# Feed-forward of a fused attention block: gate and up with the ternary weights stationary, the inner transposes gone, heads split a tile ahead, a new order on TensorE

## The reference

```python
def h_bitlinear(x, w):
    xq = act_quant(fwht(x))
    wq = weight_quant(w)
    return jnp.einsum('bsh,oh->bso', xq, wq)
gate = h_bitlinear(hidden_states, w_gate)
up = h_bitlinear(hidden_states, w_up)
return h_bitlinear(jax.nn.silu(gate) * up, w_down)
...
x = x + _L0_xattn_ref(_layernorm(x, axis=-1), ctx_1024, ...)
x = x + _L0_ffn_ref(_layernorm(x, axis=-1), ...)
```

## Time and profile before

| | |
|---|---|
| Median of 3 runs | 1412.14 us (1410.57 to 1414.44) |
| Profiled execution, own time | 1411.2 us |
| Its span | 1409.4 us |
| Mean granted TensorE clock | 0.996 |
| TensorE busy | 1378.7 us, 98% |
| VectorE, ScalarE, GpSimd busy | 934.5, 940.3, 516.6 us |

### The profile page before, as it was taken

How to read it: one execution, slowest core, us unless ns; L and a number is a source line. 1 busy time by engine, 2 the same in 40 slices (tenths; PEclk the granted TensorE clock), 3 DMA queues, 4 the chain that set the end, 5 groups by cost and what they waited for, 6 DMA issues and landing times. The chain is left out here.

```text
span 1409.4 us, 25806 instructions
## 1 busy us (share of the span) xinstructions
PE 1378.7 (98%) x8407; PEld 1187.5 (84%) x8407; DVE 934.5 (66%) x2399; ACT 940.3 (67%) x2072; POOL 516.6 (37%) x323
## 2 busy tenths in 40 slices
PE   8999988999999999999999999999989999999998
PEld 8889867999999999999999999998967676776765
DVE  5222046667777777777777777767457677776775
ACT  4566558888888888888888888888633334343332
POOL 0033324432233223332233223335544465655551
PEclk9999999999999999999999999999999999999999
DMA  7767813344433443444434444326343322233211
GB/s 234 213 180 221 232 48 90 91 122 118 130 111 116 131 130 108 112 135 117 125 108 123 125 128 124 105 82 190 123 153 88 78 61 68 61 98 75 60 30 42
DMA packets 173492, 165.05 MB, mean 117 GB/s; under 512 B 81440, under 2 KB 149040, under 8 KB 171568
## 3 DMA queue, kind: packets, MB, share of 16 engines
q1 hardware_dynamic: 166448, 150.82, 38.7%
q10 hardware_dynamic: 6912, 12.59, 2.7%
HBM read 123.44 MB, written 33.01 MB: 111 GB/s over the span
## 5 line engine op out<-in xcount | busy, mean ns | idle before, releaser
L768 POOL TENSOR_TENSOR rk_sp<-ms_sp,neg_half 76x10 f32<-76x10 f32 (+1 forms) x128 | 237.9, 1876 | 560.2 <-DMA ms_sp<-ms 560.2
L1198 DVE CUSTOM_DVE_ANT_0 sc<-psS,rk 100x361 f32<-100x361 f32 x256 | 136.5, 533 | 93.1 <-PE psS L843 71.5
L990 ACT ACTIVATE pr<-ex,ri 100x361 f32<-100x361 f32 x256 | 153.6, 600 | 63.4 <-DVE ri L1188 63.4
L983 ACT ACTIVATE ex<-sc,nb,rq_all 100x361 f32<-100x361 f32 x256 | 175.9, 687 | 5.5 <-DVE nb L1207 5.3
L871 PE MATMUL psZ<-pT_hi,cK_hi 120*128 120x400 f32 (+1 forms) x384 | 132.9, 346 | 0.0
L871 PE MATMUL psZ<-pT_hi,cK_lo 120*128 120x400 f32 (+1 forms) x384 | 131.8, 343 | 0.0
L871 PE MATMUL psZ<-pT_lo,cK_hi 120*128 120x400 f32 (+1 forms) x384 | 131.8, 343 | 0.0
L856 PEld LDWEIGHTS psP<-ident,pr 100*120 100x120 f32 (+1 forms) x768 | 80.2, 165 | 43.4 <-issue 35.3
L843 PE MATMUL psS<-ring_hi,q_hi 128*100 128x362 f32 x256 | 96.8, 378 | 4.3 <-DVE mx L1198 4.2
L856 PE MATMUL psP<-ident,pr 100*120 100x100 f32 (+1 forms) x768 | 96.5, 261 | 3.9 <-ACT pr L990 3.9
L1180 DVE TENSOR_TENSOR pT_lo<-psP,pT_hi 121x600 fp32r<-121x600 f32 x128 | 99.0, 774 | 1.5 <-ACT pT_hi L1014 1.3
(11 more groups left out here) (295 smaller groups left out, 3940.0 us busy)
## 6 DMA issues: line engine op xcount, KB each, us to landing
rk<-rk_dram SPq DMA_DIRECT2D x64, 564.1 KB
q_dram<-q_out SPq DMA_DIRECT2D x64, 200.0 KB, 4.6
q_in<-q_dram SPq DMA_DIRECT2D x64, 200.0 KB, 5.1
o_dram<-o SPq DMA_DIRECT2D x64, 200.0 KB, 5.4
stage<-in_w_ff SPq DMA_DIRECT2D x12, 1024.0 KB, 6.2
w_in<-in_w_ff ACTq DMA_DIRECT2D x48, 256.0 KB, 2.4
o_in<-o_dram SPq DMA_DIRECT2D x12, 1024.0 KB, 6.0
cT_in<-in_ctxT SPq DMA_DIRECT2D x15, 361.0 KB, 4.4
```

The source lines that it names most:

```text
L768: nc.gpsimd.tensor_tensor(rk_sp[:, cols], ms_sp[:, cols], neg_half[0:HG * SKR, :].to_broadcast([HG * SKR, n]), op=ALU.pow).then_inc(g_rk, 1)
L983: nc.scalar.activation(ex[:, h % 2, :], sc[:, h % 2, :], ACT.Exp, bias=nb[:, h % 2:h % 2 + 1], scale=factor(n), accum_out=rs[:, h % 2:h % ...
L990: nc.scalar.activation(pr[:, h, :], ex[:, h % 2, :], ACT.Copy, scale=ri[:, h % 2:h % 2 + 1]).then_inc(a_pr, 1)
L1198: nc.vector.tensor_tensor_reduce(out=sc[:, h % 2, :], in0=psS[0:SQ, 0:SK], in1=rk[:, u % 2, h, :], scale=1.0, scalar=-3.0e38, op0=ALU.mult ...
```

## The change

- **Gate and up.** The ternary weights are stationary, 128 x 128 at a time, and the 128 tokens of `q1T` move. Four matmuls of 512 columns become sixteen of 128. Hidden values now lie on the partitions and tokens along the columns, so `hidden_T` goes away. The scale of a token lies along the columns too: `al_T` transposes it (`al_rows`), ScalarE copies it to `alT`, VectorE multiplies gate by it (`gate`), ScalarE applies silu in SBUF, VectorE multiplies by up (`hidden`); the scale of up is folded into `scales2`.
- **Rotation.** `low_hT` reads `half_rot` and `hT_hi`, both in SBUF. GpSimd takes the inner rotation of blocks 0 and 1 one by one, and of the stage across only the difference of blocks 1 and 3; VectorE takes that of 0 and 2.
- **Heads.** The split of tile i+3 is used a step later: `out_high` (L1507) issues the two products with `o_hi` for heads 0 to 12 in one step and 13 to 15 in the next, `out_low` (L1514) the 16 with `o_lo` then. `low_o` waits for `v_hT`, the low parts of the hidden values of tile i+1.
- **Order.** TensorE rotates all four blocks ahead of `norm_T`; VectorE has the low parts ahead of norm and `rotate_halves`, and three peaks behind `low_xT`; GpSimd moves the residuals in the next step, after `v_q`. The fillers change.
- **Last tile.** 128 matmuls of 64 columns instead of 32 of 512 in column halves.

```diff
-        AHEAD, FIRST = 6, 10
+        AHEAD, FIRST = 13, 8
...
             def low_o(t):
                 pool.wait_ge(a_o, t + (NO - 1))
-                pool.wait_ge(v_xr, 2 * t - 2)
+                pool.wait_ge(v_hT, (t - 1) * NB)
                 nc.gpsimd.tensor_tensor(o_lo[:], o_in[:], o_hi[:].bitcast(F32), op=ALU.subtract).then_inc(g_o, 1)
...
             def rotate_across(t):
-                nc.gpsimd.tensor_tensor(half_rot[:, 2:4, :], hid[:, 0:2, :], hid[:, 2:4, :], op=ALU.subtract).then_inc(g_r2, 1)
+                nc.gpsimd.tensor_tensor(half_rot[:, 3, :], hid[:, 1, :], hid[:, 3, :], op=ALU.subtract).then_inc(g_r2, 1)
...
+                if i > -2:
+                    if 0 <= i and not last_tile(i):
+                        pool.wait_ge(v_q[1], 2 * i + 2)
+                    move_residuals(i - 1)
...
+            def out_high(t, heads):
+                if heads[0] == 0:
+                    pe.wait_ge(a_o, t + (NO - 1))
+                    pe.wait_ge(v_x1, t - 1)
+                for h in heads:
+                    for w in (wo_hi, wo_lo):
+                        nc.tensor.matmul(psA[:], o_hi[:, h, :], w[h // HALF][:, h % HALF, :],
+                                         start=(h == 0 and w is wo_hi), stop=False)
+            def out_low(t):
+                pe.wait_ge(g_o, t - 1)
+                for h in range(H):
+                    last = nc.tensor.matmul(psA[:], o_lo[:, h, :], wo_hi[h // HALF][:, h % HALF, :],
+                                            start=False, stop=(h == H - 1))
...
-                for k in range(2):
-                    for c in range(DC):
-                        last = nc.tensor.matmul(psB[:, 2 * (j % 2) + k, :], q1T[:, c, :],
-                                                wt[:, k, c, j * DIM:(j + 1) * DIM], start=(c == 0), stop=(c == DC - 1))
-                last.then_inc(p_gu, 1)
+                width, chunks = (TH, FC // 2) if last_tile(t) else (TT, FC // NB)
+                for k, done in enumerate((p_gate, p_up)):
+                    for i in range(chunks):
+                        col = (j * chunks + i) * P
+                        for c in range(DC):
+                            last = nc.tensor.matmul(psB[:, 2 * (j % 2) + k, i * width:(i + 1) * width], wt[:, k, c, col:col + P],
+                                                    q1T[:, c, 0:width], start=(c == 0), stop=(c == DC - 1))
+                    last.then_inc(done, 1)
...
-                nc.vector.tensor_tensor(hT_lo[:, n * DC:(n + 1) * DC, :].rearrange("p c t -> p (c t)"), psT[n % 2][:],
-                                        hT_hi[:, n * DC:(n + 1) * DC, :].rearrange("p c t -> p (c t)").bitcast(F32),
-                                        ALU.subtract).then_inc(v_hT, 1)
+                hi, lo = (a[:, n * DC:(n + 1) * DC, :].rearrange("p c t -> p (c t)") for a in (hT_hi, hT_lo))
+                nc.vector.tensor_tensor(lo, half_rot[:, 2 + n if last_tile(t) else n, :], hi.bitcast(F32), ALU.subtract
+                                        ).then_inc(v_hT, 1)
...
+            def gate(t, j):
+                nc.vector.tensor_tensor(sil[:, j % 2, :].rearrange("p (i t) -> p i t", t=width),
+                                        psB[:, 2 * (j % 2), :].rearrange("p (i t) -> p i t", t=width),
+                                        alT[:, 0:width].unsqueeze(1).to_broadcast([P, blocks, width]), ALU.mult).then_inc(v_g, 1)
```

More of the change, by code:

```diff
@@ L1304, in feed_forward @@
         a_o, v_o, g_o = s("a3_o"), s("v3_o"), s("g3_o")
-        p_out, p_xT, p_rx, p_q1T, p_gu, p_hT, p_rh, p_down = (
-            s(f"p3_{n}") for n in ("out", "xT", "rx", "q1T", "gu", "hT", "rh", "down"))
+        p_out, p_xT, p_rx, p_q1T, p_alT, p_gate, p_up, p_rh, p_down = (
+            s(f"p3_{n}") for n in ("out", "xT", "rx", "q1T", "alT", "gate", "up", "rh", "down"))
         v_x1, v_st, g_rs, v_xn, v_xr = (s(n) for n in ("v3_x1", "v3_st", "g3_rs", "v3_xn", "v3_xr"))
@@ L1483, in _, with first_out_proj @@
         def _(pe):
[L1484 to L1489, removed]
+            def first_out_proj(heads):
                 for h in heads:
-                    if first:
-                        pe.wait_ge(v_o, h // OH + 1)
+                    pe.wait_ge(v_o, h // OH + 1)
                     hi, lo = (w[h // HALF][:, h % HALF, :] for w in (wo_hi, wo_lo))
@@ L1648, in step @@
                         gate_up(i + 1, j)
-                if real(i + 2):
-                    out_proj(i + 2, range(FIRST if isinstance(i, int) and i == -1 else AHEAD, H))
-                if real(i + 1):
-                    hidden_T(i + 1, 0)
-                    hidden_T(i + 1, 1)
+                if isinstance(i, int) and i == -1:
+                    first_out_proj(range(FIRST, H))
+                    busy(psT[1], 8)
+                elif real(i + 2):
+                    out_high(i + 2, range(AHEAD, H))
+                    out_low(i + 2)
                 if real(i):
@@ L1669, in step @@
                 if real(i + 3):
-                    out_proj(i + 3, range(0, 4))
-                if isinstance(i, int) and i == TILES - 3:
+                    out_high(i + 3, range(3, 9))
+                elif i == TILES - 3:
                     busy(psA, 11)
@@ L1674, in step @@
                     q1_T(i + 2)
+                    al_T(i + 2)
                 if real(i + 3):
-                    out_proj(i + 3, range(4, AHEAD))
+                    out_high(i + 3, range(9, AHEAD))
+                elif i == TILES - 3:
+                    busy(psA, 3)
             busy(psT[1], 4)
@@ L1761, in step @@
                     if real(i + 1):
-                        silus(i + 1, (j,))
+                        silu(i + 1, j)
                 if real(i + 1):
-                    high_hT(i + 1, 0)
-                    high_hT(i + 1, 1)
+                    for n in range(NB):
+                        high_hT(i + 1, n)
                 if real(i + 3) and not (isinstance(i, int) and i == -2):
@@ L2019, in step @@
                 if real(i + 1):
-                    peak(i + 1, 2)
-                    peak(i + 1, 3)
+                    for n in range(1, NB):
+                        peak(i + 1, n)
                 if real(i + 2):
```

281 lines of the change are left out of this document (131 added, 150 removed).

## The result

The changed kernel takes 1489.60 us (median of 4, 1489.34 to 1495.81) against 1411.36 us of the kernel before measured beside it (1409.38 to 1414.44): a ratio of 1.0566, 95% interval 1.0552 to 1.0581. It is slower by 5.7%. The forecast was 1487. The profiled execution took 1489.68 us, with a span of 1487.9.

A forecast was written before the change was run, and what follows sets the result against it. TensorE, busy for 98% of the span, was taken as the bound. With -1.4 ahead, +5.5 first tile, +70 ten tiles, -0.4 twelfth and +2 half tile, +76 on 1411.2 gave 1487 us, range 1402 to 1500.

The forecast's parts named there:

- The added wait: Ahead of the normalised rows' transposition: GpSimd's split holds off both rotation halves, TensorE idle from 19.8 to 26.0 us.
- rival (a): The long split lets short VectorE operations through: a tile of 28.5 us, 1405 us in all; chance 0.24.
- TensorE's work: Per tile: gate and up +0.2 us, sixteen transposes leave -1.8, one for the scales +0.1; sum -1.4.
- the row of four: Four 128-column matmuls in the earlier trace, 0.40 us in all, 0.060 each; basis for taking 0.057.
- rival (c): Small gate and up matmuls cost more than 0.057 us, nothing blocks: 1450 us at 0.085 each; chance 0.05.
- VectorE's chain to the rotation: From the tile's first matmul to both rotation halves: ends at 20.5 us if unblocked, where TensorE wants them at 19.8.
- From there to the next tile: From the normalised rows' transposition to the next tile: 8.4 us, with a 0.65 us wait for the integers.
- rival (b): The split comes after the rotation anyway, as its input is late: 28.9 us a tile, 1409 us; chance 0.11.
- The clock: Half clock behind TensorE's idle time in each tile: from nothing to 3.4 us, taken as 1.7.
- The sum: Whole kernel: -1.4 ahead, first tile +5.5, ten tiles +70, twelfth -0.4, half tile +2; together +76 us, 1487 us.
- The half tile: Last half tile: 128 matmuls of 64 columns take 3.5 to 7.7 us, taken as +2.5; with -0.5 elsewhere, +2.
- The twelfth tile: The last whole tile, with no split behind it and fewer fillers: -0.4 us.

The follow-up runs named there:

- e1: The changed kernel with GpSimd's split of the heads waiting for both halves of the rotation again: 1425.43 us, ratio 1.0106.
- e2: The changed kernel with the split of the heads issued as four GpSimd operations of 512 columns: 1440.17 us, ratio 1.0209.
- e3: The kernel before, with the split of the heads waiting for the normalised rows and no longer for the rotation: 1458.09 us, ratio 1.0335.
- e9: e8 with the split of the heads waiting for the low parts of the hidden values again, as in the change: 1472.94 us, ratio 1.0445.
- e8: e7 with the second half of the hidden values' integers behind the next tile's first gate product on VectorE: 1405.40 us, ratio 0.9949.
- e4: The changed kernel with 20 unread matmuls per tile added in TensorE's wait ahead of the transposition of the normalised rows: 1478.08 us, ratio 1.0474.
- e6: e5 with 11 heads of the output projection ahead of a tile instead of 13: 1424.38 us, ratio 1.0091.
- e5: e1 with VectorE's order altered: two peaks ahead of the low parts of xT, integers q ahead of the second scales: 1426.30 us, ratio 1.0104.
- e7: e6 with VectorE's small operations for the second scales put singly between those for the first: 1410.13 us, ratio 0.9988.
- e10: e8 with al_rows behind the integers q on VectorE and its transposition behind the next heads' last four matmuls: 1403.69 us, ratio 0.9947.

## Why the prediction was right, point by point

**The added wait.** This was the main term, and its mechanism is shown: e1 takes it away by the one semaphore, e2 scales it by the length of an instruction, e3 and e9 put it into two other orders. The split was said to be in at 19.7 and to end at 24.2 us into the tile, the halves of xr at 24.5 and 26.0, as 4.5 and 1.3 of waiting. Measured in the tile from 1140.70: 24.5, 24.8 and 26.2; 4.63 and 1.48 us long. The row from which it was inferred (a pair of short rotations that ended just behind two of GpSimd's) was enough; the row against it (L1146 beside L768) says nothing of an operation with 2048 columns. The Trainium skill's page "SBUF — State Buffer" (section "SBUF: two separate sides") has the rule as an exclusive lock held for the whole instruction; the 4.63 beside 4.69 agrees with it. The rival (a), which spoke for a partial hold, is out.

**TensorE's work.** 128 matmuls in 7.20 us against a forecast of 7.3: the row of four was a fair sample. So rival (c) is out. The figure of about 81 ns on the Trainium skill's page "TensorE: Matmul & The Clock Gate" (section "Back-to-back issue gap") isn't what this stretch shows, 56 ns sustained over 128 pairs; the page's formula for a single matmul, N/2.4 + 2.5, gives an estimated 56. The saving per tile was put at 1.4 us. In e8 TensorE is busy for 28.01 of a tile's 28.67 us, in the kernel before for 29.07 of 29.10: right in kind, with 1.1 saved, 0.3 less.

**VectorE's chain to the rotation.** Put at 20.5 if unblocked; e1 has xr's end at 1175.68, 20.9 into its tile. TensorE was said to want it at 19.8; it arrives at 21.1. It waits 0.23 and 0.50 for low parts on the way, which the prediction had at nothing; the other 0.6 are tails ahead of these waits and work that its sum left out. That made the idle time 5.0 instead of 6.2, at nearly the same end, 26.2.

**From there to the next tile: this step was wrong.** "8.4" stood for transpositions, matmuls of the output projection and a wait of 0.65 for the integers. In a blocked tile at full clock (e4) it is 8.8: the wait is right, 0.53 and a tail of 0.16, and the rest is short by 0.3 in small pieces. In an unblocked tile (e1) it is 9.36 (1145.39 to 1154.75), with a wait of 1.18. Of that, 0.65 is `al_rows` held out by GpSimd's addition, and the prediction had such a hold only for operations with two inputs in SBUF. Behind this wait stands the ring that e6 brought to light: the second scales, the copy of q1T and the last integers form a queue of their own through ScalarE. The prediction followed the first integers and not the second. Hence rival (b), the case of the split behind the rotation, was priced at 1409 with a tile of 28.9, and e1, which is that case, takes 1425 with one of 30.5.

**The clock.** Taken at 1.7 us a tile, the middle of a range from nothing to 3.4, and so a guess inside its bounds. Behind the start of the transpositions a tile of the change takes 10.2 us where e4 takes 8.8: 1.4. The whole tile is 1.3 longer, since e4 starts them 0.1 later.

**The sum.** A tile was forecast as 26.0 + 8.4 + 1.7 = 36.1; measured are 26.2 + 8.8 + 1.4 = 36.4, the middle term from e4. The 0.6 that the first two are short and the 0.3 too much for the clock partly cancel; that the agreement is within 2.6 us has some luck in it.

**The half tile.** +2.5 for matmuls of 64 columns was mis-sized: to the next instruction they take 3.73, against 3.57 before, so 0.2. In their place TensorE waits 1.8 us for low parts (L1597), 0.5 before, and the stretch is 0.5 longer. The twelfth tile, put at -0.4, is +1.1. It has no split behind it; TensorE waits 0.73 there for low parts, 0.65 for xr, 0.25 for the low part of its transposition and 0.76 for q, and of these the prediction had the last, as 0.65, and 0.15 of the third.

## What to carry to other kernels

Ask of every long GpSimd operation what VectorE does with SBUF at that moment, not only whether GpSimd is free: here the result of the split was wanted a whole tile later, no engine waited for it, and starting it 1.3 us earlier in the tile (19.8 in the change, 21.1 in e1) cost 64 us. Put it where VectorE reads PSUM (the peaks), or cut it. And where an edit shortens the busiest engine by a few per cent, follow the ring of small operations through every queue before counting the gain: the first two repairs (e5, e6) moved the wait and not the time, and the two that cut the ring itself (e7, e8) took 1.75 us off a tile.

## What the runs showed of the hardware

- VectorE operations with one input in SBUF are held out as well: al_rows 0.28 alone, 0.92 to 1.32 when it meets GpSimd's addition; integers of 512 columns 0.41 alone, 0.75 to 0.80 when they do (e10). The prediction had this for two inputs only. The Trainium skill's page "SBUF — State Buffer" (section "SBUF: two separate sides") gives the same lock to VectorE's operations in a two-port mode; the held times agree with that, but no run here shows in which mode these two ran.
- Operations of VectorE with one input in PSUM go on beside the split: in e1 it runs from 1145.36 to 1149.96, and inside it L1829 (psT and an SBUF input) takes 0.69 and three peaks take 1.88, as anywhere.
- Matmuls with a weight load each are issued 56 ns apart at 128 columns and 29 ns apart at 64.
- With a wait of 3.3 us (e3) or 5.0 us (the change) in each tile the clock is granted at half for 3.4 or 6.8 us of a tile, in the change in all ten, in e3 in nine of ten, and the mean of the ten tiles is 0.95 and 0.92; in e1, e2, e4 and e8, whose longest waits in a steady tile are 1.8 us, it is 1.00.
